# The slot array cleared during the routed experts, the second-layer weights loaded one expert per step, the slot work put ahead of the attention work, and the remainder tiles moved one group later

## The chip, the cores and the metric

The kernel runs on one core of one Trainium2 chip. The metric is the device time of one launch in microseconds (us), the lower the better. The core has TensorE (PE in the profile, with its weight loads as PEld), VectorE (DVE), ScalarE (ACT), GpSimd (POOL) and SyncE (SP), and 16 DMA engines that serve all queues. The engines run side by side and meet only at semaphores.

## The reference, cut to what matters

The input is 16 sequences of 256 tokens with 256 features, 4096 tokens in all. Four residual layers follow each other:

```python
x = x + _L0_xattn_ref(_layernorm(x), ctx, ctx, ...)      # mLSTM cell, 8 heads
x = x + _L0_ffn_ref(_layernorm(x), ...)                  # 16 experts, each takes its top tokens, plus a shared expert
x = x + _L1_xattn_ref(_layernorm(x), ctx)                # linear attention, below
x = x + _L1_ffn_ref(_layernorm(x), ...)                  # 8 experts, top 2 per token, below

def _L1_xattn_ref(Q, K):
    scores = jnp.einsum('btd,bsd->bts', K, K) * mask[None, :, :]
    return Q + jnp.einsum('bts,bsd->btd', scores, Q)

def _L1_ffn_ref(x, Wg, bg, W1, b1, W2, b2, gamma, beta):
    logits = jnp.einsum('btd,de->bte', x, Wg) + bg
    top2_vals, top2_idx = jax.lax.top_k(logits, 2)
    scores = jax.nn.softmax(top2_vals, axis=-1)
    combine = jnp.einsum('btk,btke->bte', scores, jax.nn.one_hot(top2_idx, E))
    h = jax.nn.gelu(jnp.einsum('btd,edh->bteh', x, W1) + b1, approximate=False)
    y = jnp.einsum('bteh,ehd->bted', h, W2) + b2
    return _layer_norm(x + jnp.einsum('bted,bte->btd', y, combine), gamma, beta)
```

## The kernel before, in words

The kernel is one program per engine, and each is written out by hand in five stages; within a stage the order of an engine's instructions is the order of the calls in its function. Nothing is scheduled by a planner.

**Stage 1** computes the first attention and the shared expert. **Stage 2** runs the 16 routed experts of the first feed-forward. Per expert x, PE makes two projections up and one down in four parts; POOL gathers the tokens of expert x + 2 and adds the results of x - 1 into `dACC` in DRAM; SP loads the weights of expert x + 2 and, for even x, one of four pieces of `W1` of the last layer. SP runs ahead until the wait in `expert_w_in` for the third weight, whose one raw buffer is free at the end of expert x.

**Stage 3** is where most of the change lies. The 16 sequences are taken as 8 pairs (512 tokens each), and the loop over `i in STEPS` runs 11 steps (i = 0 to 10) as a pipeline: step i handles the layer norm statistics of pair i + 1 (`x_stats`, `shift`, with the reciprocal square root on POOL, `rsqrt`), its scores (`own_scores`, `mask_scores`), the attention of pair i - 1 (`attend`, `add_attention`, `z_stats`), the transposes and router logits of pair i - 2 (`z_transposed`, `logits`, `add_bias`, `pick`) and the slots of pair i - 3 (`places`, `slots`, `slots_out`). The router gives each token two experts. Each expert has a region of `dSL` in DRAM; a slot there holds a token's number and its weight. `places` counts on PE how many tokens stand ahead of each in its region, `slots` on DVE turns that into row numbers `po`, and `slots_out` on POOL writes 128 slots with each indirect DMA, eight of them per pair, 64 in all. `dSL` must be cleared before the first of them, since a tile of 256 slots may read past the end of a region; a cleared slot names one of 256 padding rows. SP loads in this stage the token tiles `x2`, the transposed context `c3T` and the eight experts' `W2` (1 MB each, to W2_AT), and stores `out`, `dZ` and `dOUT`. After the last pair, DVE works out from the counts which expert and which row each of 39 visits reads (32 full tiles, then 7 remainders, `part tiles`).

**Stage 4** makes the 39 visits in `ORDER`: 32 tiles of 256 slots and 7 remainders of 128 slots at region borders. Each visit has four units of work (two halves up, two halves down), and each needs its weights split into a high part `wh` (ACT, or DVE for the last unit) and a low part `wl` (DVE). POOL gathers the tokens and adds the results into `dOUT`; the additions of a visit wait until those of the visit before have landed. **Stage 5** is the last layer norm and the output; it begins when the last addition has landed.

## Time and profile before

| | us |
|---|---|
| median of 3 runs | 1340.76 |
| lowest and highest | 1339.64, 1347.96 |
| the profiled execution | 1333.03 |
| its span | 1331.0 |
| PE busy | 1141.8 |
| DVE busy | 927.7 |
| ACT busy | 798.7 |
| POOL busy | 662.0 |

The profile is one execution on the chip. Its times are counted from the first instruction of the span. The stages lie so: stage 1 until about 405, stage 2 until about 679, stage 3 until about 819, stage 4 from 830 to 1281, stage 5 until the end. In the table of stretches each line gives the length of the stretch, then the busy time and the number of instructions of PE, PEld, DVE, ACT and POOL, the granted TensorE clock as a share of full speed, the mean busy share of the DMA engines, and GB/s. The chain of waits is the chain of work that ended last, followed back from the end: start, length, and what it was. In a timeline a line gives start, length, engine, line of the program, operation, and in square brackets how long the engine sat idle ahead of it and what ended that. PE matmuls overlap, so their lengths add up to more than the time between starts.

### The profile page before, as it was taken

To read this page: it belongs to the slowest core of one execution; us is meant where nothing else is said; L and a number is where in the kernel's file an instruction comes from. 1 tells how busy PE (TensorE), PEld (TensorE's weight loads), DVE (VectorE), ACT (ScalarE), POOL (GpSimd) and SP (SyncE) were. 2 spreads that over 40 slices of the span, in tenths; PEclk is the share of its full clock that TensorE was granted. 3 is DMA by queue.
4 is the path that set the end of the run, shared out by engine and by line. 5 is a ranking of instruction groups with operands and counts; after the bars stand their busy time and mean duration, and the time that the engine had idled before them with its cause. 6 is when DMAs were issued, how large, how long until landed. Compare 5 with 4: busy or idle time off the path is not lost.

```text
span 1331.0 us, 23926 instructions
## 1 busy us (share of the span) xinstructions
PE 1141.8 (86%) x8296; PEld 1050.0 (79%) x8296; DVE 927.7 (70%) x2040; ACT 798.7 (60%) x1579; POOL 662.0 (50%) x586
## 2 busy tenths in 40 slices
PE   3789999898869999999966861999999999999950
PEld 2688787787758888888856751999999999999940
DVE  5677887667656665666536855787887788787857
ACT  3746656553335556565536531877778787777734
POOL 2434543343255565565333776255665645454436
PEclk8659998989989999999978865999999999999975
DMA  6544333311345666667489841244445433233249
GB/s 221 175 142 147 132 135 105 127 46 43 119 143 158 164 169 172 177 186 190 109 238 329 277 133 41 41 67 76 81 69 82 74 60 63 46 57 57 41 101 223
DMA packets 146119, 166.89 MB, mean 125 GB/s; under 512 B 28528, under 2 KB 126832, under 8 KB 143952
## 3 DMA queue, kind: packets, MB, share of 16 engines
q1 hardware_dynamic: 107680, 119.73, 27.5%
q0 software_dynamic: 35040, 42.75, 19.9%
q10 hardware_dynamic: 3280, 2.90, 0.7%
q8 instruction: 66, 1.08, 0.3%
q14 instruction: 53, 0.43, 0.1%
HBM read 114.74 MB, written 50.59 MB: 124 GB/s over the span
## 4 chain that ended last, share of the span: by engine, by line
PE 65%; DVE 13%; POOL 6%; issue 6%; ACT 5%; DMA 4%; POOLq 0%; ACTq 0%; DVEq 0%; SPq 0%
PE quad L1945 15%; PE pb L1964 13%; PE quad L1198 12%; PE pb L1213 6%; PE quad L298 4%; PE pb L352 4%; POOL dSL L1816 2%; PE pb L366 2%; DVE Dm L527 1%; DMA c3T<-in_ctxT 1%; PE pb L264 1%; ACT Dm L839 1%; PE quad L1926 1%; POOL dACC L1339 1%; PE pb L1183 1%
## 5 line engine op out<-in xcount | busy, mean ns | idle before, releaser
L2009 DVE TENSOR_TENSOR wl<-W,wh 128x1024 fp32r<-128x1024 f32 x156 | 188.2, 1227 | 78.9 <-ACT gl L2089 53.8
L2126 POOL DMA_INDIRECT dOUT<-y,es x71 | 135.2, 1904 | 197.2 <-DVE y L2041 187.5
L1964 PE MATMUL pb<-wh,hh 128*128 128x256 f32 x568 | 164.3, 289 | 0.0
L1964 PE MATMUL pb<-wh,hl 128*128 128x256 f32 x568 | 160.6, 283 | 0.0
L1964 PE MATMUL pb<-wl,hh 128*128 128x256 f32 x568 | 160.6, 283 | 0.0
L1339 POOL DMA_INDIRECT dACC<-ye,idxJ x64 | 101.8, 1590 | 102.4 <-ACT ye L1303 54.5
L2060 ACT CAST wh<-W 128x1024 fp32r x117 | 121.8, 1048 | 31.5 <-issue 19.2
L2089 ACT ACTIVATE gl<-quad,b1c 128x256 f32<-128x256 f32 (+1 forms) x312 | 124.7, 451 | 18.6 <-PE quad L1945 18.2
L1945 PE MATMUL quad<-xh,wh 128*128 128x256 f32 (+1 forms) x624 | 125.5, 283 | 7.9 <-ACT hh L2094 6.4
L1945 PE MATMUL quad<-xh,wl 128*128 128x256 f32 (+1 forms) x624 | 125.3, 282 | 0.0
L1945 PE MATMUL quad<-xl,wh 128*128 128x256 f32 (+1 forms) x624 | 125.1, 282 | 0.0
L1964 PEld LDWEIGHTS pb<-wh,hh 128*128 128x128 f32 x568 | 108.8, 192 | 0.7 <-DVE wl L2009 0.3
L1964 PEld LDWEIGHTS pb<-wl,hh 128*128 128x128 f32 x568 | 109.0, 192 | 0.0
L1964 PEld LDWEIGHTS pb<-wh,hl 128*128 128x128 f32 x568 | 108.8, 192 | 0.0
L2028 DVE TENSOR_TENSOR hl<-gl,hh 128x512 fp32r<-128x512 f32 (+1 forms) x156 | 97.0, 639 | 12.4 <-ACT hh L2094 9.0
L1945 PEld LDWEIGHTS quad<-xh,wh 128*128 128x128 f32 x624 | 97.4, 193 | 9.5 <-ACT hh L2094 7.6
L2108 POOL DMA_INDIRECT xs<-dZ,es x71 | 88.1, 1241 | 26.2 <-issue 17.7
L1297 ACT CAST ehh<-egf 128x512 fp32r<-128x512 f32 x64 | 39.7, 620 | 99.8 <-DVE egf L1247 99.8
L1945 PEld LDWEIGHTS quad<-xh,wl 128*128 128x128 f32 x624 | 97.3, 193 | 0.0
L1945 PEld LDWEIGHTS quad<-xl,wh 128*128 128x128 f32 x624 | 97.3, 193 | 0.0
L2094 ACT CAST hh<-gl 128x512 fp32r<-128x512 f32 (+1 forms) x156 | 90.9, 582 | 4.9
L1198 PE MATMUL quad<-xeh,ewh 128*128 128x512 f32 x256 | 84.5, 411 | 1.5 <-DVE xel L1241 1.5
(284 smaller groups left out, 3179.6 us busy)
## 6 DMA issues: line engine op xcount, KB each, us to landing
MB<-dM SPq DMA_DIRECT2D x16, 1024.0 KB, 5.3
W<-in_W SPq DMA_DIRECT2D x16, 1024.0 KB, 10.7
wraw<-in_Wg SPq DMA_DIRECT2D x16, 512.0 KB, 6.4
wraw<-in_Wu SPq DMA_DIRECT2D x16, 512.0 KB, 7.7
wraw<-in_Wd SPq DMA_DIRECT2D x16, 512.0 KB, 5.3
b2c<-in_b SPq DMA_DIRECT2D x39, 128.0 KB, 3.2
xp<-in_x SPq DMA_DIRECT2D x16, 256.0 KB, 5.5
cT<-in_ctxT SPq DMA_DIRECT2D x16, 256.0 KB, 4.8
```

The source lines that it names most:

```text
L1198: ins = pe.matmul(bank.t[:, :], a_[m][x % 2][:, 512 * k + 128 * f:512 * k + 128 * f + 128], b_[x % 2][:, k, :], start=n == 0, stop=n == 5)
L1213: ins = pe.matmul(bank[:, 0:256], a_[x % 2][:, f, 128 * tt:128 * tt + 128], b_[2][x % 2][:, 256 * f:256 * f + 256], start=n == 0, stop=n = ...
L1339: g.indirect_dma_start(out=dACC[:, :], out_offset=bass.IndirectOffsetOnAxis(ap=idxJ[:, tt, x:x + 1], axis=0), in_=ye[x % 2][:, tt, :], in_ ...
L1945: ins = pe.matmul(bank[:, TS * c:TS * c + width(i)], ww[:, k, fs], xx[i % 2][:, k, 0:width(i)], start=m == 0, stop=m == 5)
L1964: ins = pe.matmul(bank.t[:, 0:256], a_[s][:, c, 128 * tt:128 * tt + 128], b_[n % 3][:, 256 * c:256 * c + 256], start=half == 0 and m == 0, ...
L2009: v.tensor_tensor(w_dst(wl[n % 3], kind), w_src(expert(i), kind, half), w_dst(wh[n % 3], kind), ALU.subtract).then_inc(*v_t.up("w", n))
L2028: v.tensor_tensor(hl[hidden(i, half)][:, 2 * q_:2 * q_ + 2, w], gl[(2 * (2 * i + half) + q_) % 3][:, :, w], hh[hidden(i, half)][:, 2 * q_: ...
L2060: a.copy(w_dst(wh[n % 3], kind), w_src(expert(i), kind, half)).then_inc(*a_t.up("w", n))
L2089: ins = a.activation(g_[:, c, 0:width(i)], ab4.of(i, half, q_)[:, TS * c:TS * c + width(i)], ACT.Gelu, bias=b1c[i % 6][:, cc:cc + 1])
L2094: a.copy(hh[hidden(i, half)][:, 2 * q_:2 * q_ + 2, 0:width(i)], g_[:, :, 0:width(i)]).then_inc(*a_t.up("hh", i, half, q_))
L2108: g.indirect_dma_start(out=xs[i % 3][:, c, :], out_offset=None, in_=dZ[:, :], in_offset=bass.IndirectOffsetOnAxis(ap=es[i % 6][:, c, 1:2]. ...
L2126: g.indirect_dma_start(out=dOUT[:, :], out_offset=bass.IndirectOffsetOnAxis(ap=es[i % 6][:, tt, 1:2].bitcast(U32), axis=0), in_=y1[i % 2][ ...
```

## The change

There are four parts.

1. `dSL` is no longer cleared by ACT's queue at the start of stage 3. POOL and DVE prepare the cleared pattern in stage 2 (experts 1 and 3), and SP issues the transfer in the loop's pass for expert 5, in pieces of 512 bytes per descriptor instead of 1024; the array has 35840 rows instead of 36864. ACT's two writes of the padding rows of `dOUT` and `dZ` stay where they were, under a semaphore of their own.
2. `W2` is loaded one expert per step (steps 0 to 7) instead of 3, 2, 2 and 1 in steps 0 to 3.
3. In stage 3 the slots of pair i - 3 go first in step i: on PE `places` ahead of `attend`, on DVE `slots` right behind `x_stats`, on POOL four of the eight writes between the two reciprocal square roots and four behind the second. Small tables that DVE made before its first work now come behind the first `shift`.
4. In `ORDER` each remainder comes four tiles later, so the last visit is a remainder of 128 slots.

```diff
-SLROWS = (E1 * REG + TS + 2047) // 2048 * 2048
+SLROWS = (E1 * REG + TS + 1023) // 1024 * 1024
...
@@ sp_stage2
+                if x == 5:
+                    sp.wait_ge(*v_sl.of("empty"))
+                    sp.dma_start(dSL.rearrange("(k p j) e -> p k (j e)", p=128, j=8),
+                                 slz[:, :, :].rearrange("p j e -> p (j e)").unsqueeze(1).to_broadcast([128, SLROWS // 1024, 128])
+                                 ).then_inc(*init_st.up("slots", by=16))
...
-            if t % 4 == 3 and t // 4 < PARTS:
-                ORDER.append(FULL + t // 4)
+            if t % 4 == 3 and t > 3:
+                ORDER.append(FULL + t // 4 - 1)
...
@@ pe_stage3
             for i in STEPS:
+                if at(i - 3) is not None:
+                    places(i - 3)
                 if at(i - 1) is not None:
                     attend(2 * i - 2)
                     attend(2 * i - 1)
-                if at(i - 3) is not None:
-                    places(i - 3)
...
@@ dve_stage3
                 if at(i + 1) is not None:
                     x_stats(i + 1)
+                if at(i - 3) is not None:
+                    slots(i - 3)
                 if at(i - 1) is not None:
                     add_attention(2 * i - 2)
                     add_attention(2 * i - 1)
                     z_stats(i - 1)
                 if at(i + 1) is not None:
                     shift(xsm[(i + 1) % 2], "x", i + 1)
-                if at(i - 3) is not None:
-                    slots(i - 3)
                 if at(i - 1) is not None:
                     shift(zsm[(i - 1) % 2], "z", i - 1)
...
@@ act_stage3
-            a.wait_ge(*v_r3.of("slz"))
-            a.dma_start(dSL.rearrange("(k p j) e -> p k (j e)", p=128, j=16),
-                        slz[:, :, :].rearrange("p j e -> p (j e)").unsqueeze(1).to_broadcast([128, SLROWS // 2048, 256])).then_inc(*init_st.up("slots", by=16))
...
@@ pool_stage3
             for i in STEPS:
-                if at(i - 4) is not None:
-                    slots_out(i - 4, 3)
                 if at(i + 1) is not None:
                     rsqrt(xsm[(i + 1) % 2], "x", i + 1)
+                if at(i - 3) is not None:
+                    slots_out(i - 3, 0)
+                    slots_out(i - 3, 1)
                 if at(i - 1) is not None:
                     rsqrt(zsm[(i - 1) % 2], "z", i - 1)
                 if at(i - 3) is not None:
-                    for c in range(3):
-                        slots_out(i - 3, c)
-            slots_out(PAIRS - 1, 3)
-            for s in sx_st:
-                g.wait_ge(*s.all())
+                    slots_out(i - 3, 2)
+                    slots_out(i - 3, 3)
...
@@ sp_stage3
-            W2_AT = {0: (0, 1, 2), 1: (3, 4), 2: (5, 6), 3: (7,)}
+            W2_AT = {x: (x,) for x in range(E1)}
```

On POOL in steps 4 and 5 of stage 3 (`xsm` and `zsm` hold the statistics of the two layer norms, `dSL<-en` are slot writes) there stood before:

```order
L1808 TENSOR_TENSOR xsm<-xsm,mhalf 128x4
L1808 TENSOR_TENSOR zsm<-zsm,mhalf 128x4
L1816 DMA dSL<-en,po 36864x16 x8
L1808 TENSOR_TENSOR xsm<-xsm,mhalf 128x4
L1808 TENSOR_TENSOR zsm<-zsm,mhalf 128x4
```

and in the same place of the changed kernel:

```order
L1816 TENSOR_TENSOR xsm<-xsm,mhalf 128x4
L1825 DMA dSL<-en,po 35840x16 x4
L1816 TENSOR_TENSOR zsm<-zsm,mhalf 128x4
L1825 DMA dSL<-en,po 35840x16 x4
L1816 TENSOR_TENSOR xsm<-xsm,mhalf 128x4
```

The eight writes that stood in one block between `zsm` and the next `xsm` are now split into four and four.

On DVE at the start of step 3 and later ones (L1550 and L1557 are the first and last of the statistics, L1577 adds the attention, L1623 to L1643 are the slots, `S` is the masking of scores) there stood before:

```order
L1557 TENSOR_SCALAR xsm<-xsm 128x4
L1577 TENSOR_TENSOR x<-x,quad 128x512 x2
L1550 BN_STATS zsm<-x 128x6 x4
L1554 BN_AGGR zsm<-zsm 128x2 x4
L1557 TENSOR_SCALAR zsm<-zsm 128x4
L1562 TENSOR_SCALAR xsm<-xsm 128x4
L1563 SCALAR_TENSOR_TENSOR xsm<-xsm 128x4
L1623 TENSOR_SCALAR rt<-rt 128x4
L1625 SCALAR_TENSOR_TENSOR rt<-io8f,pb 128x32
```

and now:

```order
L1563 TENSOR_SCALAR xsm<-xsm 128x4
L1629 TENSOR_SCALAR rt<-rt 128x4
L1631 SCALAR_TENSOR_TENSOR rt<-io8f,pb 128x32
L1636 COPY en<-tok 128x8
L1638 RECIPROCAL en<-rt 128x4
L1640 TENSOR_TENSOR rt<-rt 128x64
L1643 TENSOR_TENSOR en<-rt,en 128x4
L1646 TENSOR_REDUCE rt<-rt 128x4 x2
L1649 CAST po<-rt 128x8
L1583 TENSOR_TENSOR x<-x,quad 128x512 x2
```

The slots moved from behind the second statistics and the `shift` of x to ahead of the addition of the attention.

## Rows read from the trace of the kernel before

**Rows 1.** Stretches: stage 2, stage 3, and ten microseconds within it.
```profile
405.00:644.80 239.80, 239.80 (x1423) 213.17 (x1422) 148.11 (x205) 142.48 (x260) 139.24 (x102) 1.00 0.67 175
678.90:818.60 139.70, 84.60 (x434) 74.40 (x434) 92.77 (x487) 62.24 (x123) 78.35 (x80) 0.74 0.69 227
750.00:760.00 10.00, 7.35 (x40) 6.48 (x41) 9.41 (x56) 7.39 (x15) 7.21 (x8) 0.88 0.58 186
```
**Rows 2.** The chain of waits: start, length, what; start and end of stage 3.
```profile
678.86 8.24 DMA x<-dACC
...
816.48 2.10 DMA dSL<-en,po
```
**Rows 3.** Issue to landing in stage 3: loads and stores of x2, then `dSL` cleared.
```profile
DMA to landing us min/median/max: 4.1/7.0/12.8
...
DMA to landing us min/median/max: 13.3/13.3/13.3
```
**Rows 4.** What ended PE's idle time ahead of its score matmuls: us, times.
```profile
  DMA c3T<-in_ctxT: 7.7, 2
```
**Rows 5.** Timeline of POOL in stage 3.
```profile
723.84 1.06 POOL L1816 DMA_INDIRECT dSL<-en,po  x1 [0.89 <-DVE po L1643]
...
751.05 1.00 POOL L1808 TENSOR_TENSOR zsm<-zsm,mhalf 128x4 f32<-128x4 f32 x1 [0.68 <-DVE zsm L1557]
...
764.84 1.04 POOL L1816 DMA_INDIRECT dSL<-en,po  x1 [0.54 <-DVE po L1643]
...
768.71 0.96 POOL L1816 DMA_INDIRECT dSL<-en,po  x1 [0.31 <-issue]
...
773.76 0.96 POOL L1816 DMA_INDIRECT dSL<-en,po  x1 [0.30 <-issue]
```
**Rows 6.** Timeline of DVE in stage 3, first rows of work in steps 3 to 7.
```profile
716.52 1.41 DVE L1550 BATCH_NORM_STATS2 xsm<-x 128x6 f32<-128x256 f32 x4
...
756.04 1.41 DVE L1550 BATCH_NORM_STATS2 xsm<-x 128x6 f32<-128x256 f32 x4
...
757.97 1.28 DVE L1577 TENSOR_TENSOR x<-x,quad 128x512 f32<-128x512 f32 x2
...
763.51 0.17 DVE L1623 TENSOR_SCALAR rt<-rt 128x4 f32<-128x4 f32 x1
...
764.38 0.17 DVE L1643 CAST po<-rt 128x8 uint32<-128x8 f32 x1
...
768.51 1.28 DVE L1577 TENSOR_TENSOR x<-x,quad 128x512 f32<-128x512 f32 x2
```
**Rows 7.** Timeline of PE in stage 3, step 5 and the last transposes.
```profile
745.73 0.38 PE L1503 MATMUL pb<-rt,stri 128*128 128x32 f32 x2 [0.36 <-DVE before L1617]
...
746.17 1.07 PE L1483 MATMUL pb<-ident,z 128*128 128x128 f32 x8
...
751.41 0.68 PE L1470 MATMUL quad<-Q,S 128*128 128x256 f32 x2
...
753.65 0.59 PE L1472 MATMUL quad<-Q,S 128*128 128x256 f32 x2
...
790.91 1.95 PE L1483 MATMUL pb<-ident,z 128*128 128x128 f32 x8
```
**Rows 8.** Timeline of DVE, end of stage 3: last `po`, last entry of visits.
```profile
802.16 0.17 DVE L1643 CAST po<-rt 128x8 uint32<-128x8 f32 x1
...
814.53 0.36 DVE L1710 TENSOR_SCALAR te<-codi 128x7 int32<-128x7 int32 x1
```
**Rows 9.** Timeline of SP (its DMA issues) in stage 2, experts 5 and 6.
```profile
512.47 0.47 SPq L1359 DMA_DIRECT2D wraw<-in_Wu  x1
529.06 0.37 SPq L1359 DMA_DIRECT2D wraw<-in_Wd  x1
```
**Rows 10.** Who waited for whom on PE in stage 4: total, times, longest.
```profile
PE quad L1945 <- ACT hh L2094: 6.4, 7, 1.4
```
**Rows 11.** The chain of waits at the end of stage 4: start, length, what.
```profile
1284.59 3.73 DMA dOUT<-y,es
```

More of the change, by code:

```diff
@@ L1164, in build @@
         ye = M2.ring("ye", 2, [128, 4, D])
+        sli = M2.sb("sli", [128, 8], I32)
+        slz = M2.sb("slz", [128, 8, 16])
         ew_ld = [ring(f"expert_w{m}_loaded", (2, 2, 1)[m]) for m in range(3)]
@@ L1269, in dve_stage2 @@
                     w_low(x + 1, 2)
+                if x == 3:
+                    v.wait_ge(*sl_g.of("rows"))
+                    v.tensor_scalar(sli[:, :], sli[:, :], TS - 1, None, ALU.bitwise_and).then_inc(*v_sl.up("in tile"))
+                    v.wait_ge(*v_sl.of("in tile"))
+                    v.tensor_scalar(slz[:, :, 1:2].bitcast(I32), sli[:, :].unsqueeze(2), N, None, ALU.add).then_inc(*v_sl.up("empty"))
         def act_stage2(a):
@@ L1349, in pool_stage2 @@
                     gather(x + 2)
+                if x == 1:
+                    g.memset(slz[:, :, :], 0.0)
+                    g.iota(sli[:, :], [[1, 8]], base=0, channel_multiplier=8).then_inc(*sl_g.up("rows"))
                 if x:
@@ L1426, in build @@
         ln_ld, beta_st = sig("final_w_loaded"), sig("beta_added")
-        r3_ld, w2_ld, init_st = sig("top2_w_loaded"), sig("w2_loaded"), sig("slots_cleared")
+        r3_ld, w2_ld, init_st, pad_st = sig("top2_w_loaded"), sig("w2_loaded"), sig("slots_cleared"), sig("pads_cleared")
+        sl_g, v_sl = sig("pool_empty_slots"), sig("dve_empty_slots")
         ct_ld = ring("ctxT_loaded", 2)
@@ L1528, in dve_stage3 @@
             for m, t in ((0, tri), (1, ones), (2, tri)):
-                v.tensor_copy(mask3[:, m, :], t[:, 0:128])
-            v.wait_ge(*c3_g.of("iota"))
-            v.tensor_scalar(sli[:, :], sli[:, :], TS - 1, None, ALU.bitwise_and).then_inc(*v_r3.up("sli"))
-            v.wait_ge(*v_r3.of("sli"))
-            v.tensor_scalar(slz[:, :, 1:2].bitcast(I32), sli[:, :].unsqueeze(2), N, None, ALU.add).then_inc(*v_r3.up("slz"))
-            v.tensor_copy(io8f[:, :], io8[:, :])
-            v.tensor_scalar(t256[:, :], ti[:, :], float(TS), None, ALU.mult).then_inc(*v_r3.up("tables"))
-            v.wait_ge(*v_r3.of("tables"))
-            v.tensor_scalar(cn[:, 4, :], io8f[:, :], -1.0, 7.0, ALU.mult, ALU.add)
-            v.tensor_scalar(cn[:, 5, :], io8f[:, :], 65536.0 + REG, None, ALU.mult).then_inc(*v_r3.up("codes"))
-            v.wait_ge(*v_r3.of("codes"))
+                ins = v.tensor_copy(mask3[:, m, :], t[:, 0:128])
+            ins.then_inc(*v_r3.up("masks"))
+            v.wait_ge(*v_r3.of("masks"))
             def mask_scores(b):
@@ L1649, in dve_stage3 @@
             shift(xsm[0], "x", 0)
+            v.wait_ge(*c3_g.of("iota"))
+            v.tensor_copy(io8f[:, :], io8[:, :])
+            v.tensor_scalar(t256[:, :], ti[:, :], float(TS), None, ALU.mult).then_inc(*v_r3.up("tables"))
+            v.wait_ge(*v_r3.of("tables"))
+            v.tensor_scalar(cn[:, 4, :], io8f[:, :], -1.0, 7.0, ALU.mult, ALU.add)
+            v.tensor_scalar(cn[:, 5, :], io8f[:, :], 65536.0 + REG, None, ALU.mult).then_inc(*v_r3.up("codes"))
+            v.wait_ge(*v_r3.of("codes"))
             for i in STEPS:
@@ L1812, in slots_out @@
                     g.wait_ge(*init_st.all())
+                    g.wait_ge(*pad_st.all())
                 if c == 0:
```

6 lines of the change are left out of this document (1 added, 5 removed).

## The prediction, made before the change was run

> **What bounds the kernel now.** I read the table of stretches first, then the chain of waits through stage 3, then the timelines of POOL, DVE and PE there.
>
> In stage 2 PE is busy for all of 239.8 us out of 239.8 [rows 1]. Whatever is put beside it there costs nothing unless it makes PE wait. Stage 3 is different: 139.7 us in which no engine is full (DVE 92.8, PE 84.6, POOL 78.4), the TensorE clock is at 0.74 on average, and the DMA engines are 0.69 busy. So it is bound by waits between engines, and the order of work decides. It begins with a wait of 8.24 us for the first load of x and ends 2.10 us after the last slot write was issued at 816.48 [rows 2], at 818.6.
>
> Between these, three limits take turns. Until about 740 it is partly data: PE sits 7.7 us in two places until transposed context has landed [rows 4]. After that POOL is nearly continuous: eight slot writes take from 764.84 to 774.72, 9.9 us, and with the two square roots of 1.0 us and the gap ahead of the block of 0.2 to 0.5 us a step is some 12.4 us of POOL work [rows 5]. Last comes the tail, in which the last pair goes from its square root through every engine once.
>
> **The change part by part.**
>
> *Clearing in stage 2.* The new transfer is issued behind the load at 512.47 and ahead of the one at 529.06 [rows 9], which must wait for a raw buffer anyway. It has some 16 us before anyone stands behind it. The same transfer took 13.3 us in stage 3 [rows 3], with the DMA engines full; here they are 0.67 busy [rows 1]. POOL and DVE are 0.58 and 0.62 busy in that stretch and their few instructions are under 3 us together. I take 0, with 0 to 5 us as the bounds (5: the gathers or weights of one expert come late by a third of those 13.3 us). If PE had no such cover, up to 13.3 us would show.
>
> *The start of stage 3.* The first load of x loses its competitor. It took 8.24 us; the quickest transfer of this size and kind in the stage took 4.1 [rows 3]. Two writes of padding rows remain, so I take 4.8, a gain of 3.4 us (bounds 0 and 4.1). Against it, four small DVE table operations move from idle time into the chain behind the first `shift`; the nearest row is 0.17 us for one of such size [rows 6], partly overlapped: +0.5 us (bounds 0 and 0.7). Steps 0 to 2 keep their order and had no data wait in the rows that I read, so they shift as a block.
> The Trainium skill (DMA: Bandwidth & Descriptors, section on queues, rings and completion order) says that each DMA engine takes turns between the queues that have work. By that rule alone the load would take half of 8.24, 4.1 us, and the start would gain 4.1 instead of 3.4. The row of 4.1 agrees.
>
> *Spread weights.* The 7.7 us of waits for context [rows 4] should go. This lies inside the stretch from step 3 to step 7, which runs from 716.52 to 768.51, 52.0 us for four steps [rows 6]. What is late next is the loop below.
>
> *Slots first.* Here the new order closes a tighter ring between DVE and POOL. Counted from the end of the square root of z on POOL (751.05 + 1.00 = 752.05) DVE shifts, masks, adds the bias, picks, and begins the next statistics at 756.04: 3.99 us. The statistics of x take 757.97 - 756.04 = 1.93. POOL then takes 0.1 to start and 1.0 for the square root of x; meanwhile DVE does the slots (763.51 to 764.55, 1.04 us), so they are ready. A gap of 0.3, four slot writes (764.84 to 769.67, 4.83 us), and the square root of z again, 1.0. Sum: 3.99 + 1.93 + 0.1 + 1.0 + 0.3 + 4.83 + 1.0 = 13.2 us [rows 5, 6]. Before, the whole block of eight writes stood between z and x and covered DVE's 5.9 us; now only four do, 5 us with the gap, and POOL idles about 1 us per step. So the new step is about 13.2 us, against POOL's own 12.4.
> PE must fit in. From `places` at 745.73 to the start of `attend` at 751.41 it needs 5.7 us, and `attend` another 2.8, to 754.24, so 8.5 us at full clock [rows 7]. But now `places` waits for the pick of the same pair and `attend` stands behind it, so both begin only with the step; before, `attend` ran ahead in the time of the pick. PE must reach the end of the logits by about 10.3 us of the step. It has about 4.5 us of idle time ahead of each step, and the rows show what idle time does: the same eight transposes took 1.07 us at 746.17 and 1.95 us at 790.91 [rows 7], and the granted clock is 0.88 in 750 to 760 [rows 1], a mix of the levels 2.4 and 1.2 GHz. A slow beginning eats the margin of 1.8 us. I add 0.3 us per step: 13.5, four steps 54.0, so +2.0 us against 52.0. Bounds: POOL's 12.4 four times, -2.4; and a PE at the low level through `places`, `attend` and transposes, +10 (below).
>
> *The tail.* From step 7 at 768.51 to the last `po` took 33.8 us and the tables another 12.6, to 814.89 [rows 6, 8]; POOL ended later, at 818.6. Now steps 7 and 8 are bound by PE: `places`, `attend` and transposes at the low clock 8.2 (4.1 doubled), logits about 2, then bias and pick 2.95 (the 3.99 above less the shift and the two maskings), 13.1 us each. After those 26.2 us come `places`, 1.1, and what took 11.4 us before, from the last transposes at 790.91 to the last `po` at 802.33 [rows 7, 8]: 38.7 us, and the tables at 51.3. POOL has its last eight writes left at 38.7 and is done at about 50. Before it was 50.1 in all (818.6 - 768.5). So +1.2 us (bounds -2.5, PE at full clock, and +5), and the end of the stage moves from the last slot write to DVE's tables.
>
> *Remainder last.* Each of the 7 remainders costs PE a wait of about 0.9 us for ACT [rows 10], wherever it stands. The last visit being short, one addition instead of two ends it, but that addition must wait until those of the full visit before have landed (3.73 us for the last to land [rows 11]), which start 4.3 us (three short units instead of three long ones) nearer to the end. That cancels. I take 0, bounds -2 and +1.
>
> Sum: 0 - 3.4 + 0.5 + 2.0 + 1.2 + 0 = **+0.3 us**. The sum is against the profiled execution, 1333.03 us (span 1331.0 and 2 around it), which lies 7.7 us under the median of the runs, 1340.76. I carry the difference over to the median: **1341 us**. A measurement of this kernel can tell about 1% from no change, 13 us.
>
> **The rivals.**
>
> *POOL stays the bound.* If the loop hides behind POOL, the writes start at 716.5 - 2.9 + 3.5 = 717.1 instead of 723.84, and 64 writes of 1.265 us, nine square roots of 1.05 and 2.1 to landing end at about 808.4: 10.2 us less, **1331 us**. For it: POOL's continuous stretch before. Against it: the sum of 13.2, each part of which is a row. It would need the pick to be over sooner than any row shows.
>
> *PE becomes the bound at the low clock (slower).* If `places`, `attend` and transposes all run at 1.2 GHz (0.4, 2.8 and 0.9 doubled, 8.2 us) and the rest at full (4.3), the logits end at 12.6 and the step takes 12.6 plus the 3.0 for bias and pick, 15.6 us: +2.4 over 13.2 in four steps, and about 4 more in the tail. That is 12 to 13 us over the forecast, **1354 us**. It decides as soon as PE loses more than 1.8 us per step to the clock. For it: the transposes at 1.95, and longer idle time ahead of each step. Against: the clock recovers inside a step in the rows of 750 to 760.
> The Trainium skill (TensorE: Matmul & The Clock Gate, part 1) states that the throttled clock is the default and that activity releases it, which speaks against an order that gives PE a longer pause in each step. Taken strictly it gives this rival's time; the mean clock of 0.88 shows that it doesn't hold for a whole step.
>
> *The clearing hurts stage 2.* Weights or gathered tokens late at one expert: 5 us, **1346 us**. Against: the 16 us of room.
>
> *The change doesn't do what it says at the start.* If the first load is slow for another reason, the 3.4 us stay away: **1345 us**.
>
> **How the numbers follow.** My forecast has 0.62 (its own range 1335 to 1347, from the bounds of the start, of 0.3 us per step and of the tail). POOL as the bound 0.15, PE at the low clock 0.12, stage 2 0.05, no gain at the start 0.06. The range 1331 to 1352 takes in the forecast, POOL as the bound and the two small cases, and leaves out the far half of the slow clock. Faster by over 1% needs the end of the first rival and more, below 1327.4: 0.08. Slower by over 1%, above 1354: 0.08. Within 1%: 0.84.
>
> **What would show it.** The first statistics of x should start 3 to 4 us earlier against the last scatter; the waits for context should be gone; DVE steps 3 to 6 should be 13.2 to 14 us apart, with POOL idle about 1 us ahead of each square root of x, ended by DVE; the granted clock from 715 to 770 should fall below that of before; the last visit entry (DVE), not the last slot write, should release SP; stage 2 should keep PE full; remainder waits should be six or seven of 0.9 us. Steps of 12.4 us with POOL never idle would prove the loop wrong, and steps of 15 us with DVE waiting for logits would prove the slow PE right. A stage 4 that is longer by several us would mean that I misread the remainders.

## The result, and the profile after

| | us |
|---|---|
| kernel before, median of 12 runs beside the change | 1343.05 (1339.64 to 1347.96) |
| changed kernel, median of 12 runs | 1333.43 (1328.46 to 1338.13) |
| ratio | 0.9919, 95% interval 0.9900 to 0.9937 |
| profiled execution of the change, its span | 1336.25, 1334.4 |

The change gains 0.8%. I had forecast no change, 1341 us. The time lies in my range and within 1%, but the gain is outside the error of the measurement. Against the one profile of before (1333.03 us) the profile after is 3 us *slower*, against the runs the change is 10 us faster. That contradiction is what the experiments look into.

The table of stretches of the changed kernel answers to [rows 1]: length, busy time and instructions of PE, PEld, DVE, ACT, POOL, granted clock, DMA share, GB/s.

```profile
405.00:644.80 239.80, 239.80 (x1425) 213.23 (x1423) 148.49 (x208) 142.47 (x260) 137.61 (x102) 1.00 0.70 185
677.00:823.30 146.30, 85.94 (x425) 76.01 (x423) 92.30 (x486) 60.03 (x121) 79.45 (x86) 0.70 0.64 202
750.00:760.00 10.00, 6.90 (x34) 6.10 (x33) 7.30 (x44) 6.22 (x13) 7.11 (x8) 0.66 0.86 288
```

Stage 2 with the clearing in it keeps PE busy for all of 239.8 us. Stage 3 is longer than the 139.7 of the profile before, its clock lower (0.70 for 0.74), and 0.66 in place of 0.88 in 750 to 760.

The start, in the timelines of POOL (the last addition of stage 2) and DVE (the first statistics), against [rows 2]:

```profile
674.78 1.54 POOL L1346 DMA_INDIRECT dACC<-ye,idxJ  x1 [0.31 <-issue]
...
682.57 1.41 DVE L1556 BATCH_NORM_STATS2 xsm<-x 128x6 f32<-128x256 f32 x4 [6.58 <-DMA x<-dACC]
```

7.8 us from one to the other; the profile before has 12.1 (675.02 to 687.13).

One step of the new loop on DVE, then the next statistics, against [rows 6]:

```profile
727.60 1.41 DVE L1556 BATCH_NORM_STATS2 xsm<-x 128x6 f32<-128x256 f32 x4
...
731.50 0.69 DVE L1583 TENSOR_TENSOR x<-x,quad 128x512 f32<-128x512 f32 x1 [0.92 <-PE quad L1486]
733.24 0.69 DVE L1583 TENSOR_TENSOR x<-x,quad 128x512 f32<-128x512 f32 x1 [1.05 <-PE quad L1486]
...
741.38 1.41 DVE L1556 BATCH_NORM_STATS2 xsm<-x 128x6 f32<-128x256 f32 x4
```

13.78 us per step, with two waits for PE's `attend` (L1486), 2.0 us together, that no step of before has. On POOL, against [rows 5]:

```profile
743.49 1.06 POOL L1816 TENSOR_TENSOR xsm<-xsm,mhalf 128x4 f32<-128x4 f32 x1 [1.28 <-DVE xsm L1563]
744.74 1.03 POOL L1825 DMA_INDIRECT dSL<-en,po  x1 [0.20 <-issue]
...
749.86 1.04 POOL L1816 TENSOR_TENSOR zsm<-zsm,mhalf 128x4 f32<-128x4 f32 x1 [0.29 <-DVE zsm L1563]
...
757.20 1.06 POOL L1816 TENSOR_TENSOR xsm<-xsm,mhalf 128x4 f32<-128x4 f32 x1 [1.28 <-DVE xsm L1563]
```

POOL waits 1.28 us for DVE ahead of each square root of x, as forecast. The tail, against [rows 8]: the last bias, the last `po`, and the last entry of visits.

```profile
802.92 0.19 DVE L1593 TENSOR_TENSOR lg<-pb,bgr 128x32 f32<-128x32 f32 x1 [6.39 <-PE pb L1509]
...
810.57 0.17 DVE L1649 CAST po<-rt 128x8 uint32<-128x8 f32 x1
...
823.18 0.17 DVE L1723 TENSOR_SCALAR te<-codi 128x7 int32<-128x7 int32 x1
```

Stage 4, against [rows 10] and [rows 11]: PE's wait for ACT, and the last two pieces of the chain there.

```profile
PE quad L1952 <- ACT hh L2101: 6.0, 6, 1.6
```

```profile
1283.56 3.73 DMA dOUT<-y,es
1288.02 3.75 DMA dOUT<-y,es
```

From the last matmul to the last layer norm it is 8.7 us; before, 10.1.

Stage 3 of all profiles, in us. *Start* runs from the last addition to the first statistics of x, *to step 3* and *3 to 7* to the ends of the picks that begin those steps, *tail* from step 7 to the last `po`, *last pick* is the distance of the last two picks, *total* from the last addition to stage 4's first matmul with weights. Chips are given letters; "before" is the median of the kernel before on the same chip in the same comparison. The first profile of before and the first of the changed kernel come without a chip. The five stretches are read from one profile each, median and ratio from all runs; the ratios stand as on record and are not the quotients of the two medians (for e11 that quotient is 0.9982). Outside *total* the profiles spend between 1167.4 us (e7) and 1179.8 us (e15), in no order of kernels, so a single profile's total foretells the runs only to some microseconds.

| kernel | chip | before | median | ratio (95%) | start | to step 3 | 3 to 7 | tail | last pick | total |
|---|---|---|---|---|---|---|---|---|---|---|
| before, first profile | | | | | 12.1 | 29.4 | 52.0 | 33.9 | 10.2 | 154.8 |
| e1 before | A | 1345.06 | 1344.36 | 1.0005 (0.9976-1.0034) | 12.2 | 29.8 | 53.4 | 49.8 | 17.9 | 169.3 |
| e5 before | B | 1347.12 | 1338.92 | one run | 12.1 | 29.8 | 53.4 | 46.7 | 13.6 | 166.2 |
| e15 before | D | 1343.11 | 1349.43 | one run | 12.1 | 30.4 | 54.4 | 46.6 | 17.5 | 167.6 |
| changed | | 1343.05 | 1333.43 | 0.9919 (0.9900-0.9937) | 7.8 | 31.3 | 54.9 | 42.0 | 13.7 | 159.8 |
| e16 changed | D | 1343.11 | 1332.33 | 0.9926 (0.9894-0.9957) | 7.6 | 31.5 | 55.1 | 40.3 | 10.4 | 158.4 |
| e11 changed | C | 1332.70 | 1330.35 | 1.0001 (0.9981-1.0022) | 7.8 | 30.3 | 53.8 | 38.0 | 10.1 | 154.2 |
| e2 part 1 | A | 1345.06 | 1341.13 | 0.9970 (0.9944-0.9997) | 7.7 | 30.3 | 53.3 | 49.5 | 17.9 | 165.5 |
| e3 parts 1, 2 | A | 1345.06 | 1336.39 | 0.9950 (0.9920-0.9980) | 9.0 | 29.7 | 52.9 | 43.5 | 15.2 | 159.8 |
| e4 part 3 | A | 1345.06 | 1341.96 | 0.9963 (0.9939-0.9987) | 12.1 | 29.6 | 56.6 | 40.6 | 10.3 | 163.0 |
| e8 part 4 | B | 1347.12 | 1344.75 | 0.9978 (0.9956-1.0000) | 12.1 | 29.9 | 53.4 | 46.4 | 13.6 | 166.0 |
| e10 parts 1, 2, 4 | C | 1332.70 | 1324.74 | 0.9951 (0.9928-0.9974) | 7.7 | 30.4 | 48.4 | 33.8 | 10.2 | 148.0 |
| e14 parts 1, 2, 4 | D | 1343.11 | 1333.91 | 0.9940 (0.9914-0.9966) | 7.7 | 30.3 | 50.6 | 44.6 | 16.9 | 157.8 |
| e7 attend first | B | 1347.12 | 1329.61 | 0.9890 (0.9859-0.9922) | 7.7 | 29.9 | 53.9 | 40.9 | 10.1 | 157.3 |
| e12 attend first | C | 1332.70 | 1326.34 | 0.9960 (0.9937-0.9983) | 8.0 | 30.2 | 53.2 | 34.5 | 10.1 | 150.0 |
| e18 attend first | B | 1346.23 | 1331.67 | 0.9892 (0.9852-0.9931) | 8.3 | 30.1 | 53.2 | 36.7 | 10.1 | 153.5 |
| e6 half the writes | B | 1347.12 | 1325.16 | 0.9827 (0.9784-0.9870) | 12.1 | 29.6 | 51.0 | 29.9 | 10.1 | 147.0 |
| e9 half, POOL busy | C | 1332.70 | 1325.21 | 0.9951 (0.9928-0.9974) | 8.7 | 32.1 | 48.8 | 32.2 | 10.2 | 146.9 |
| e13 half, POOL busy | D | 1343.11 | 1324.05 | 0.9876 (0.9841-0.9910) | 8.6 | 32.2 | 48.5 | 32.3 | 10.2 | 146.4 |
| e17 pauses | B | 1346.23 | 1337.94 | 0.9925 (0.9896-0.9954) | 7.8 | 30.0 | 53.5 | 35.0 | 10.2 | 159.7 |

### The profile page after: what moved, and what is told of

It reads as the page before. It is cut to its first block, busy times and chain, and to the rows that moved or that the text cites. A ratio compares the mean times of both kernels' runs of the same rounds, so it can differ in the third digit from the quotient of the medians.

```text
span 1334.4 us, 23927 instructions
## 1 busy us (share of the span) xinstructions
PE 1144.8 (86%) x8296; PEld 1054.1 (79%) x8296; DVE 929.7 (70%) x2040; ACT 798.7 (60%) x1579; POOL 658.5 (49%) x586
## 4 chain that ended last, share of the span: by engine, by line
PE 69%; DVE 15%; issue 6%; ACT 5%; POOL 3%; DMA 1%; ACTq 0%; DVEq 0%; POOLq 0%
PE quad L1952 16%; PE pb L1971 13%; PE quad L1200 13%; PE pb L1215 7%; PE quad L298 5%; PE pb L352 4%; PE pb L366 2%; ACT Dm L839 2%; DVE Dm L527 2%; PE pb L264 1%; PE quad L1933 1%; PE pb L1185 1%; PE quad L1484 1%; POOL fsm L2246 1%; DVE fsm L2187 1%
## 5 line engine op out<-in xcount | busy, mean ns | idle before, releaser
L2096 ACT ACTIVATE gl<-quad,b1c 128x256 f32<-128x256 f32 (+1 forms) x312 | 124.5, 450 | 19.5 <-PE quad L1952 16.9
L2035 DVE TENSOR_TENSOR hl<-gl,hh 128x512 fp32r<-128x512 f32 (+1 forms) x156 | 97.0, 640 | 12.2 <-ACT hh L2101 8.9
```

Source lines behind the costliest of these rows:

```text
L2035: v.tensor_tensor(hl[hidden(i, half)][:, 2 * q_:2 * q_ + 2, w], gl[(2 * (2 * i + half) + q_) % 3][:, :, w], hh[hidden(i, half)][:, 2 * q_: ...
L2096: ins = a.activation(g_[:, c, 0:width(i)], ab4.of(i, half, q_)[:, TS * c:TS * c + width(i)], ACT.Gelu, bias=b1c[i % 6][:, cc:cc + 1])
```

## The experiments

### Is the first profile of before typical? The kernel before again, and each part alone

**e1**, nothing edited.

> The kernel before, unchanged, as a control of the profile. Theory A (the profiled execution of before was a quick one, and its typical execution loses more in stage 3 while the DMA engines are full): a ratio of 1.000, a profiled span of 1336 to 1344, and stage 3 longer than 139.7 us, with waits for transposed context of more than 7.7 us. Theory B (stage 3 of before is always as profiled and the change gains in stage 4 or at the end): ratio 1.000, stage 3 within 1 us of 139.7, and the rest of the span longer in stage 4 or 5.

**e2**, part 1 alone: the hunks of the change with `SLROWS`, `sli`, `slz` and `init_st`. DVE's small tables, `W2`, the order of stage 3 and `ORDER` are as before.

> Only part 1 of the change (the slot array cleared in stage 2; W2, the order of stage 3 and the visits as before). Theory A: the first load of x lands 3 to 4 us earlier and 2.3 MB less compete with the steps, so 4 to 7 us less than before, ratio 0.995 to 0.997. Theory B: 3 us or less, ratio 0.998.

**e3**, parts 1 and 2:

```diff
-            W2_AT = {0: (0, 1, 2), 1: (3, 4), 2: (5, 6), 3: (7,)}
+            W2_AT = {x: (x,) for x in range(E1)}
```

> Parts 1 and 2 (clearing in stage 2 and W2 one expert per step), with the order of stage 3 and of the visits as before. Theory A: no wait for context is left, and POOL's slot writes bound the steps at 12.4 us: 12 to 16 us less than before, ratio 0.988 to 0.991, so faster than the whole change. Theory B: 4 us less, ratio 0.997.

**e4**, part 3 alone: the hunks of the change in the loops of PE, DVE and POOL over `STEPS`, and DVE's small tables behind the first `shift`.

> Only part 3 (slots first on PE, DVE and POOL), clearing, W2 and visits as before. Theory A: the tighter ring of DVE and POOL costs its 13.7 us per step on top of the data waits: 3 to 6 us slower than before, ratio 1.002 to 1.005. Theory B (the order itself gives the gain, since the slot writes start earlier): 3 to 6 us faster, ratio 0.996 to 0.998.

What they showed: the profile of e1 has a span of 1342.7 us, 11.7 over the first one, and 15.9 of difference in the tail alone (49.8 for 33.9). Theory A held in its ratio, span and longer stage 3, but its reason did not: the wait for context is 4.9 us, not more than 7.7. Part 1 takes its 4.4 us from the start and leaves the tail as it was (e2). Parts 1 and 2 together, and part 3 alone, each shorten the tail by 6 to 9 us against e1, though none was meant to. e3 was expected 12 to 16 us under before and came 8.7 under it; its tail still has 43.5 us. e4 was expected slower by theory A and came 3 us faster: its steps are longer as theory A says (56.6 for 53.4), and the tail pays more than that back.

Where the tail goes wrong is visible on e1's last pair. PE's last logits, POOL's slot writes beside them, and DVE's bias, which needs only those logits:

```profile
798.99 3.55 PE L1495 MATMUL pb<-w1r,zT 128*128 128x8 f32 x16 [0.97 <-ACT zT L1760]
```

```profile
802.46 0.96 POOL L1816 DMA_INDIRECT dSL<-en,po  x1 [0.30 <-issue]
...
807.52 0.96 POOL L1816 DMA_INDIRECT dSL<-en,po  x1 [0.30 <-issue]
808.78 0.96 POOL L1816 DMA_INDIRECT dSL<-en,po  x1 [0.31 <-issue]
```

```profile
808.21 0.19 DVE L1587 TENSOR_TENSOR lg<-pb,bgr 128x32 f32<-128x32 f32 x1 [10.93 <-remote]
```

The matmuls end at 802.5 and the bias starts at 808.21, 5.7 us later, while POOL issues a write every 1.27 us, the last one after the bias has started; the profile finds no engine that released it and writes "remote". The same place in the first profile of before, with POOL writing just as densely:

```profile
793.62 3.55 PE L1495 MATMUL pb<-w1r,zT 128*128 128x8 f32 x16 [0.77 <-ACT zT L1760]
```

```profile
796.04 0.96 POOL L1816 DMA_INDIRECT dSL<-en,po  x1 [0.30 <-issue]
797.30 0.96 POOL L1816 DMA_INDIRECT dSL<-en,po  x1 [0.31 <-issue]
```

```profile
797.21 0.19 DVE L1587 TENSOR_TENSOR lg<-pb,bgr 128x32 f32<-128x32 f32 x1 [5.10 <-PE pb L1495]
```

Ended at 797.17, taken up at 797.21. So PE's semaphore increment reached DVE at once in one profile and 5.7 us late in the other. The ends of matmuls are modelled in the profile, so a late end of PE would look alike; but the traces also record the increments themselves, this one at 797.19 in the first profile and at 808.19 in e1, and DVE waits late for its own increments too, where no matmul is involved. The changed kernel's profile shows this on its last pair. It has no wait called "remote", but its last logits end at 801.58, the bias follows 1.3 us later, and four additions of DVE, each of which needs only the one before, take 2.8 us:

```profile
805.27 0.17 DVE L1623 TENSOR_TENSOR before<-before,rt 128x8 f32<-128x8 f32 x1
806.47 0.17 DVE L1623 TENSOR_TENSOR before<-before,rt 128x8 f32<-128x8 f32 x1 [1.04 <-DVE before L1623]
807.18 0.17 DVE L1623 TENSOR_TENSOR before<-before,rt 128x8 f32<-128x8 f32 x1 [0.54 <-DVE before L1623]
807.87 0.17 DVE L1623 TENSOR_TENSOR before<-before,rt 128x8 f32<-128x8 f32 x1 [0.52 <-DVE before L1623]
```

In e11, where nothing is late, the same four take 0.77 us. These two delays are most of the 3.6 us between the last picks of the two profiles (13.7 and 10.1). The Trainium skill (Perfetto Trace Analysis, Per-engine timelines) says that the time in which a semaphore update becomes visible to other engines lies outside the profiled window; this trace agrees, since the 5.7 us stand in no engine's row.

### Do the slot writes hold the increments back? Half of them, and other tests

**e5**, nothing edited, for a third profile.

> The kernel before once more, for a further profile. Theory C (in a typical execution of before the end of stage 3 is held up by semaphore increments that arrive late while POOL writes slots without a pause; the profile of before that the prediction used happened to be free of it): from the end of the pick of pair 4 to the last slot numbers about 50 us, with picks 17 to 20 us apart twice. Theory D (that hold-up is an accident of two profiles): 34 us, as in the first profile.

**e6**, the kernel before without the slots of the second expert:

```diff
-                for k in range(2):
+                for k in range(1):
```

> The kernel before, but each slot write for a token's second expert is left out (32 instead of 64 indirect writes in stage 3; the second expert's part of the result is then missing, the number of visits is the same). Theory C: POOL has pauses, the increments arrive in time, picks of the last pairs 10 to 12 us apart, the stretch from pick 4 to the last slot numbers 30 to 36 us instead of 50, and the steps before it 10.5 us instead of 12.5: 20 to 28 us less than before, ratio 0.979 to 0.985. Theory D, or the low TensorE clock as the cause: the steps gain the same 8 us, but the tail stays at 44 us or more, so 8 to 14 us in all, ratio 0.990 to 0.994.

**e7**, the changed kernel with PE's order as before:

```diff
                 if at(i - 1) is not None:
                     attend(2 * i - 2)
                     attend(2 * i - 1)
+                if at(i - 3) is not None:
+                    places(i - 3)
```

and `places` taken away from ahead of `attend`.

> The changed kernel with PE's old order (attend ahead of places), everything else changed. Theory of the prediction (PE's places-first order delays the addition of the attention and eats the margin): steps 3 to 6 of 13.3 us instead of 13.7, the tail some 3 us shorter, 3 to 5 us less than the changed kernel, ratio to before 0.988 to 0.990. Rival (the DVE and POOL ring alone sets the step, and PE is covered): the same as the changed kernel, ratio 0.992.

**e8**, part 4 alone (the two lines of `ORDER`).

> Only part 4 (each remainder four tiles later, the last visit short). Theory of the prediction: nothing, ratio 0.999 to 1.001. Rival (one addition less at the end shows): the stretch from the last matmul to the last layer norm 1 to 2 us shorter than 9.7 us, ratio 0.998 to 0.999.

What they showed: e5 and e8 have tails of 46.7 and 46.4, so the first profile's 33.9 was the exception. The delay does not fall on the same increment each time: on the last pair of e5 and e8 the bias is only 1.2 us late, and the longest "remote" wait is one of ACT for PE's transposes, 7.1 us in both. With half the writes the tail is 29.9 and no wait is "remote". But e6 also halves POOL's work, so it does not say which counts. e8 gains 0.7 us between the last matmul and the last layer norm (9.0 for 9.7 in e1 and e5) and its ratio just reaches 1, so part 4 alone is not told from nothing by the runs. e7 met its expectation (0.9890); why PE's order matters is under e12.

### POOL's backlog or the writes themselves, and do the parts add?

**e9**, as e6 with POOL kept busy:

```diff
+                n = 1 + 4 * p + c
+                g.tensor_tensor(fil[:, :, n:n + 1], fil[:, :, 0:1], mhalf[:, :].unsqueeze(1).to_broadcast([128, 4, 1]), ALU.pow)
```

> The kernel before with every second slot write replaced by a square root of 128x4 on POOL on a spare tile (1.0 us, as the row of zsm at 751.05), so that POOL is nearly as busy as before (1.26 + 1.05 us in place of 2.53) while half as many writes are in flight. The slots of the second expert are left out. Theory 'completions' (increments of other engines arrive late while slot writes land back to back; e1 showed 6 us between the last logits and the bias on DVE): no late increments, the time from step 7 to the last po near the 29.9 us of e6 and at most 34, ratio 0.983 to 0.987. Theory 'backlog' (POOL's own queue of 64 writes is the bound, and the square roots stand behind it): POOL's work is down by only 8%, so the stretch stays at 43 to 49 us, ratio 0.995 to 1.0. In between (36 to 42 us): both have a share, to be split by that.

**e10**, the changed kernel with the order of stage 3 as before (the reverse of e4's edit).

> The changed kernel with the order of stage 3 as before: parts 1, 2 and 4 alone. Theory 'the writes' (the new order and the spread weights take away the same loss, each by thinning the slot writes or the data waits): as e3 plus 0.7 to 1 us from part 4, so 0.993 to 0.996, span about 1334, within 3 us of the changed kernel. Rival 'the order is what gains' (part 3 adds its 5 us to those of parts 1 and 2 and the profile of e3 was quick by chance): 0.996 to 0.999, 4 us or more above the changed kernel on the same chip. Start 7.7 to 9 us in both.

**e11**, the changed kernel, nothing edited.

> The changed kernel again, unaltered, beside the others on one chip. Expected 0.992 (0.990 to 0.994), span 1332 to 1336; from step 7 to the last po 40 to 44 us if the 42.0 of the first profile was typical. If that stretch is 46 us or more the gain of the tail was an accident of one profile, as the 33.9 of the kernel before was.

**e12**, the edit of e7.

> The changed kernel with PE's attention ahead of the places, as e7, now beside the changed kernel on one chip. If PE's order cost 0.5 us per step in steps 3 to 7 (waits of DVE for the attention, 0.9 and 1.0 us per step) and more behind them: 0.988 to 0.991, 2 to 5 us under the changed kernel of this call. If e7 was only a better chip: the same as the changed kernel within 1 us.

What they showed was not what they were for. On this chip the kernel before itself takes 1332.70 us (35 runs), 10 to 14 less than on the others, and the changed kernel gains nothing that its interval tells from zero: 1.0001, with medians 2.35 us apart. None of the four profiles has a "remote" wait after step 7. e9 therefore had no loss to take away and decides nothing. e11's expectation (0.990 to 0.994) failed, and e12's ratio (0.988 to 0.991) with it, though e12 is 4.0 us under the changed kernel as expected. e10's ratio lies where it was expected, but not its distance from the changed kernel, which was to be within 3 us: without part 3 the kernel is 5.6 us *quicker* than with it, 3 to 7 takes 48.4 for 53.8 and the tail 33.8 for 38.0.

e12 against e11 shows PE's share in that. DVE's statistics and the addition behind them, e11:

```profile
736.52 1.41 DVE L1556 BATCH_NORM_STATS2 xsm<-x 128x6 f32<-128x256 f32 x4
739.89 0.69 DVE L1583 TENSOR_TENSOR x<-x,quad 128x512 f32<-128x512 f32 x1 [0.39 <-PE quad L1486]
741.63 0.69 DVE L1583 TENSOR_TENSOR x<-x,quad 128x512 f32<-128x512 f32 x1 [1.05 <-PE quad L1486]
```

and e12, attention first on PE:

```profile
739.54 1.41 DVE L1556 BATCH_NORM_STATS2 xsm<-x 128x6 f32<-128x256 f32 x4
742.42 1.28 DVE L1583 TENSOR_TENSOR x<-x,quad 128x512 f32<-128x512 f32 x2
```

Both additions now run together without a wait.

### On a chip with the loss

**e13** is e9's kernel, **e14** e10's, **e15** the kernel before, **e16** the changed kernel.

> As e9: every second slot write replaced by a square root on POOL, the slots of the second expert left out. e9 met a chip on which the kernel before itself runs in 1332.7 us and has no late increments to take away, so it decided nothing. On a chip where the kernel before takes 1340 us or more: theory 'completions' expects the whole loss gone, ratio 0.981 to 0.986 and 30 to 34 us from step 7 to the last po, as e6; theory 'backlog' expects 0.992 to 1.0 and 43 us or more. On a chip where before takes 1335 us or less: 0.995 again.

> Parts 1, 2 and 4, as e10, which gave 0.9951 on the quicker chip and there beat the changed kernel by 5.6 us. On a chip where before takes 1340 us or more: theory 'the new order protects against late increments' expects this kernel at or above the changed one (1334 to 1338, ratio 0.993 to 0.996), with 43 us or more from step 7 to the last po; rival 'the order is never worth anything' expects it 4 us or more below the changed kernel there too. On a quick chip: as e10, 33.8 us and 5 us below the changed kernel.

> The kernel before, unaltered, one profile on the same chip as the three others. On a chip where before takes 1340 us or more: 46 to 50 us from step 7 to the last po; on one where it takes 1335 us or less: 33 to 35 us, as the profile that the prediction was made on. If a slow chip shows 34 us there, the tail is not where the chips differ.

> The changed kernel beside them. If its gain is there only where increments come late: on a chip where before takes 1340 us or more, ratio 0.990 to 0.994 and 40 to 43 us from step 7 to the last po; on a quick chip 0.998 to 1.002 and 37 to 39 us, as e11. If the ratio of 0.992 was an accident of one chip: 1.0 on both.

This chip has the loss (before 1343.11), and all four tails came out as the theory of the writes has them; of the ratios only e13's is off, 0.9876 where 0.981 to 0.986 was expected. e15, last pair, PE, POOL, DVE:

```profile
804.67 3.55 PE L1495 MATMUL pb<-w1r,zT 128*128 128x8 f32 x16 [0.77 <-ACT zT L1760]
```

```profile
812.22 0.96 POOL L1816 DMA_INDIRECT dSL<-en,po  x1 [0.30 <-issue]
813.49 0.96 POOL L1816 DMA_INDIRECT dSL<-en,po  x1 [0.30 <-issue]
820.91 0.95 POOL L1816 DMA_INDIRECT dSL<-en,po  x1 [6.46 <-DVE cn L1681]
```

```profile
815.59 0.19 DVE L1587 TENSOR_TENSOR lg<-pb,bgr 128x32 f32<-128x32 f32 x1 [12.42 <-remote]
```

The logits end at 808.2. POOL is in a run of sixteen writes, the last one at 813.49; DVE moves at 815.59, 7.4 us late. That the run is over by then is not the rule: in e14 the last bias comes 3.9 us late at 798.77 and POOL writes on until 801.58. In e13 POOL is never idle either, but a square root stands behind each write:

```profile
787.71 1.03 POOL L1818 DMA_INDIRECT dSL<-en,po  x1 [0.20 <-issue]
788.77 1.05 POOL L1821 TENSOR_TENSOR fil<-fil,mhalf 128x4 f32<-128x4 f32 x1
790.02 1.03 POOL L1818 DMA_INDIRECT dSL<-en,po  x1 [0.20 <-issue]
```

```profile
790.83 0.19 DVE L1588 TENSOR_TENSOR lg<-pb,bgr 128x32 f32<-128x32 f32 x1 [5.10 <-PE pb L1496]
```

PE's row (787.24, 3.55 long) ends at 790.79, and DVE starts at 790.83. The tail is 32.3 us here and 32.2 on chip C: the chips differ by 10 us with the dense writes and by 1.2 (1324.05 and 1325.21) without. POOL's backlog is ruled out: a write and a square root cost POOL 2.31 us here, two writes cost it 2.53 before, and the tail is 32.3 for 46.6. The waits of e14 that no engine ended, after 760: total, times, longest.

```profile
ACT zT L1768 <- remote: 11.1, 3, 5.9
DVE lg L1598 <- remote: 8.9, 1, 8.9
```

e10, the same kernel on chip C, has none, and 10.8 us less in its tail.

Where the change gains on this chip can be read from e15 and e16: start -4.5, to step 3 +1.1, 3 to 7 +0.7, tail -6.3, in total -9.2 us; the medians are 10.8 apart. e14 without the new order has -9.8 in total and 9.2 in the medians.

### The run of writes or their number? And the best version

**e17**, e14's kernel with a pause behind every fourth write of pairs 4 to 6:

```diff
+                if c % 2 and 4 <= p <= 6:
+                    n = 1 + 2 * (p - 4) + c // 2
+                    g.tensor_tensor(fil[:, :, n:n + 1], fil[:, :, 0:1], mhalf[:, :].unsqueeze(1).to_broadcast([128, 4, 1]), ALU.pow)
```

> Parts 1, 2 and 4 (the kernel of e14) with all 64 writes, and one square root of 128x4 on a spare tile (1.05 us) on POOL behind every fourth slot write of pairs 4 to 6, six of them. Theory 'the unbroken run of writes holds increments back' (e14: DVE began the bias 3.9 us behind the last logits, e15 7.5 us, amid runs of 16 writes 1.27 us apart): a pause now comes every four writes, so no wait is longer than 4 writes, 5 us, and most are gone; on a chip where before takes 1340 us or more the stretch from step 7 to the last po falls from 44.6 to 35 to 40 us and the kernel is 3 to 7 us below e14, at 1327 to 1331 us. Rival 'only the number of writes counts': it stays at 43 to 46 us and 1334 us or more. On a quick chip 2 to 5 us worse than e10, since six square roots are 6.3 us of POOL in a tail that ends with POOL there.

**e18**, the edit of e7.

> The changed kernel with PE's attention ahead of the places, as e7 and e12. e7 gave 1329.6 us (0.989) on a chip with the loss, e12 1326.3 us (0.996) on the quicker one. Expected again 0.988 to 0.991 where before takes 1340 us or more, 34 to 41 us from step 7 to the last po, at least 2 us below the changed kernel's 1332 to 1333 us; if it is at 1332 us or above there, its lead in e7 was chance.

e17's tail is 35.0 us with all 64 writes in place; e14's on chip D is 44.6, e5's and e8's on e17's own chip are 46.7 and 46.4, and e10, on the chip without the loss, has 33.8. POOL, then DVE, which starts 0.04 us behind logits that end at 798.26:

```profile
796.92 0.96 POOL L1825 DMA_INDIRECT dSL<-en,po  x1 [0.30 <-issue]
798.19 0.96 POOL L1825 DMA_INDIRECT dSL<-en,po  x1 [0.30 <-issue]
799.17 1.05 POOL L1829 TENSOR_TENSOR fil<-fil,mhalf 128x4 f32<-128x4 f32 x1
...
822.90 0.96 POOL L1825 DMA_INDIRECT dSL<-en,po  x1 [0.30 <-issue]
```

```profile
798.30 0.19 DVE L1599 TENSOR_TENSOR lg<-pb,bgr 128x32 f32<-128x32 f32 x1 [5.08 <-PE pb L1510]
```

So the number of writes alone does not make the loss. That it is the unbroken run is likely and not shown. For it: e17 still has a "remote" wait in its tail, where eight writes stand in a row as before; PE's transposes end at 771.6 and ACT takes them up at 774.17. Against it: in e7 POOL has a square root at 777.68 and then only four writes, the last at 782.78, and still the bias is 4.4 us late, at a time when POOL has nothing to issue:

```profile
785.08 0.19 DVE L1593 TENSOR_TENSOR lg<-pb,bgr 128x32 f32<-128x32 f32 x1 [6.15 <-remote]
```

And in e16 the last logits end amid eight writes in a row and the bias follows after 0.04 us. All of this is one profile of each kernel, and e14's kernel was not run on e17's chip. The time did not follow: the last write is issued at 822.90, 7.0 us after the last entry of visits, where in e14 it comes 3.3 us before it. POOL became the end of the stage, and the kernel was no quicker (0.9925; e14 on another chip 0.9940). My expectation of 1327 to 1331 us was wrong, because I did not add the six pauses to POOL's own chain. e18 held in its ratio, 0.9892, as e7, and in its tail (36.7), but its 1331.67 us is not the 2 us under the changed kernel's 1332 to 1333 that I had expected.

The changed kernel with PE's attention first beats the kernel before on both chips that it ran on: 0.9890 and 0.9892 on chip B, 0.9960 on C. The changed kernel itself stood beside it only on C, 4.0 us slower; on B it was not run, and its 0.9919 and 0.9926 from elsewhere lie within the intervals. Without the new order at all (e10, e14) the ratios are 0.9951 on C and 0.9940 on D, so that version is at least as good where the loss is absent; beside it on a chip with the loss it was not run.

## Why the prediction was wrong, by its own steps

**The step that failed: "I carry the difference over to the median", with the tail's 33.8 us.** The 7.7 us between the profiled execution and the median were treated as a constant beside the sum. They were a loss in the very stretch that I costed. Four other profiles of before or of e8's kernel, on three chips, have 46 to 50 us from step 7 to the last `po`; the changed kernel has 40 to 42 there. I forecast that this stretch grows from 33.8 to 38.7 us, and the way from step 7 to the end of the stage by 1.2. On chip D, with both kernels profiled, it fell from 46.6 to 40.3, and the way to DVE's last table from 59.0 to 52.9. With the sum of +0.3 on the profile's own 1333.03 I would have written 1333.3, which is what the runs gave, but not for a reason of mine: it is so because the change takes away most of a loss that this profile did not have.

On the terms themselves, the chip without the loss (C) is the fair test, and there the forecast of no change holds (1.0001, interval 0.9981 to 1.0022). No profile of before exists from C; the first one stands in for it:

- *Clearing in stage 2:* forecast 0; PE full for 239.8 of 239.8 us. Right.
- *Start:* forecast -3.4; measured -4.3 (12.1 to 7.8), and e2 shows it alone with -0.3% in the runs. The load itself takes 3.9 us in e11. The Trainium skill (DMA: Bandwidth & Descriptors, section on queues, rings and completion order), whose taking of turns gave 4.1, agrees with this better than my 4.8 us for the load. DVE's tables cost nothing visible at the start. But steps 0 to 2 did not shift as a block: *to step 3* is 0.9 us longer in e11 than in the first profile, 1.1 longer in e16 than in e15, and no run says why.
- *Spread weights:* the 7.7 us of waits for context are gone, but a typical profile of before has one of 4.9 (e1). With parts 1 and 4, and without the new order, the stretch 3 to 7 is 48.4 on C against 52.0 in the first profile, and 50.6 against 54.4 on D; on A, with part 1 (e3), it hardly fell, 52.9 against 53.4.
- *Slots first:* forecast 13.5 per step and 54.0 for four; measured 13.8 and 54.9, and 53.8 in e11. Right in size. The +0.3 that I gave to PE's clock came as DVE's waits for `attend` (0.92 and 1.05 us), which stands behind `places`; e12 removes them and three of the four steps are 13.2, the ring's sum to a tenth.
- *Tail without the loss:* forecast 38.7 and the tables at 51.3; e11 has 38.0 and 50.6. The stage ends with DVE's tables, 3.3 us after the last write is issued; that the tables end it was forecast.
- *Remainder last:* forecast 0, bounds -2 and +1; -0.7 (e8) to -1.4 us. Six waits for ACT of 1.0 us each.

**The rivals.** POOL as the bound: refuted, POOL waits 1.28 us in each step. Its time (1331) came out near for another reason. Its sum was also wrong: 717.1 us, 64 writes of 1.265, nine square roots of 1.05 and 2.1 give 809.6, not 808.4. PE at the low clock: the clock fell to 0.66 in 750 to 760, but steps are 13.8, not 15.6. Stage 2 hurt, and no gain at the start: both refuted. The case that happened, increments held back and a change that loses less to them, was not among them, and no row of the profile that I had showed it. What I could have seen is that the profiled execution was below the lowest of the runs, 1339.64.

**What the change really does** then depends on the chip. Without the loss: -4.3 for the start, some -3.6 for the weights, -1 for the remainder, and for the order 5.4 us from step 3 to 7 and 4.2 in the tail (e11 less e10), of which 6.2 reach the end of the stage (*total* 154.2 less 148.0), because the last slot write no longer ends it. That leaves some -3, near the 2.35 us between the medians. With it, the order pays part of its cost back: e16 and e14 are within 2 us of each other, and the tail is 40.3 for 44.6. Why it does is not shown. In steps 3 to 6 four writes and a square root take turns in place of eight writes in a row, but in the tail no square root of x is left, and POOL issues eight in a row there too (e16, 790.39 to 799.23).

**Still open:** what passes the increments on and why chips differ. The traces differ in one more thing: those of the four kernels on C and the first one of before record 15,680 to 16,202 semaphore updates by engines and DMAs, all others 13,091 to 13,737, e6 and e13 included, which have no late increments in stage 3. Whether updates go unrecorded there or are joined, and whether recording them has a part in the delay, no run tells; each run on record comes with a traced span. Whether the first profile of before was taken on a chip like C is inferred from its time, its tail and this count, not known. Chip B had the loss in two comparisons, C was met once, and no comparison showed a chip change its kind.

## What to carry to other kernels

Before a sum is built on a profile, compare its time with every run shown: where it lies outside them, the difference belongs to some stretch, and it must not be added as a constant. A wait that the profile puts down to nobody while the awaited engine's row has ended, and a chain of small operations of one engine that suddenly has gaps of 0.5 to 1 us, are signs of late increments; look at what POOL issues in those microseconds. Fewer slot writes took the delays away in e6 and e13. Pauses between them shortened the tail in e17, but as filler they cost as much at POOL's end. Measure on more than one chip before calling 0.8% a gain or a loss.

## What the runs showed of the hardware that I had not expected

- On three of four chips semaphore increments became visible late in and just behind the microseconds in which POOL issued indirect writes 1.26 us apart: PE's last one 3.9, 5.7 and 7.4 us late in e14, e1 and e15, but 0.04 or 0.05 us in e4, e16 and e18 with writes as dense. DVE's own increments were 0.5 to 1.0 us late in the changed kernel's profile.
- With a square root of 1.05 us behind each of half as many writes (e13) nothing was late in stage 3. With one behind every fourth write of three pairs (e17) the last increment took 0.04 us.
- On the fourth chip the same runs of writes delayed nothing, and the same kernel was 10 to 14 us quicker (1332.70 against 1343.11 to 1347.12).
- Halving the writes was worth 1.7% on a chip with the loss (e6) and, with POOL kept busy, 0.5% on the one without (e9).
